# GpSimd weighs five of every eight units of the prior attention, VectorE three, in a fused attention and mixture-of-experts kernel

## What is computed

```python
use_sparse = lam >= SPARSE_THRESHOLD                      # one flag for each of the 2 samples
scores = jnp.einsum('bhqd,bhkd->bhqk', Q, K) * scale
bias = lam[:, None, None, None] * where(prior_mask, 0.0, -1.0)
dense_out = einsum('bhqk,bhkd->bhqd', softmax(scores + bias), V)
...                                                       # the same over 32 listed keys of each query
sparse_out = einsum('bhsk,bhskd->bhsd', softmax(s_scores), Vg)
out = where(use_sparse, sparse_out, dense_out)
```

## Time and profile before

| | us |
|---|---|
| median of 3 runs | 1601.72 |
| lowest and highest | 1598.1, 1601.99 |
| the profiled execution | 1594.84 |
| its span | 1593.0 |

### The profile page before, as it was taken

One profiled execution on the slowest core, in us unless ns is written; L12 is line 12 of the kernel. 1 busy time (PEld: TensorE's weight loads), 2 busy tenths in 40 slices (PEclk: granted clock), 3 DMA queues, 4 the chain that ended last, 5 costly groups with the idle time before them and its releaser, 6 DMA issues. The chain is left out here.

```text
span 1593.0 us, 21701 instructions
## 1 busy us (share of the span) xinstructions
PE 1455.9 (91%) x7649; PEld 693.1 (44%) x7697; DVE 1032.9 (65%) x2506; ACT 810.3 (51%) x975; POOL 666.1 (42%) x455
## 2 busy tenths in 40 slices
PE   4788999999999999888998878799999999999988
PEld 2513333332433332333343323345566567777745
DVE  8789878889767886665877493554451437667232
ACT  3753666787556666457765657733332134334101
POOL 5336799998769999613312012141000300000160
PEclk9759999999999999999999979799999999999999
DMA  2340010231311111113242022130000223544061
GB/s 80 122 132 9 27 41 29 89 80 56 80 34 47 38 39 27 35 35 83 91 115 74 21 71 71 55 101 3 1 0 24 93 70 111 177 153 135 28 121 28
DMA packets 74759, 104.52 MB, mean 66 GB/s; under 512 B 14843, under 2 KB 49092, under 8 KB 74650
## 3 DMA queue, kind: packets, MB, share of 16 engines
q1 hardware_dynamic: 70730, 96.66, 20.1%
q0 software_dynamic: 3072, 6.03, 1.9%
q10 hardware_dynamic: 848, 0.43, 0.1%
HBM read 72.39 MB, written 32.77 MB: 66 GB/s over the span
## 5 line engine op out<-in xcount | busy, mean ns | idle before, releaser
L1475 ACT ACTIVATE sb_prob<-wide,sb_ranges 128x1024 f32<-128x1024 f32 (+3 forms) x384 | 380.1, 1006 | 207.8 <-PE wide L2218 114.5
L1249 POOL TENSOR_TENSOR sb_prob<-sb_prob,sb_weight 128x1024 f32<-128x1024 f32 x192 | 448.9, 2363 | 73.1 <-ACT sb_prob L1475 70.9
L2213 PE MATMUL wide<-sb_stack_q,sb_stack_k 114*128 114x512 f16 (+3 forms) x896 | 282.4, 364 | 15.6 <-ACT sb_prob L1475 7.7
L1799 DVE CUSTOM_DVE_ANT_0 sb_junk<-bank,sb_bias 128x512 bf16<-128x512 f32 x345 | 230.4, 687 | 54.0 <-PE bank L2183 49.2
L1522 ACT ACTIVATE sb_sil<-wide,sb_weight 128x320 f32<-128x320 f32 (+1 forms) x128 | 77.5, 607 | 316.0 <-PE wide L2299 259.1
L2183 PE MATMUL bank<-sb_stack_k,sb_stack_q 112*128 112x512 f16 (+3 forms) x601 | 217.2, 378 | 20.5 <-DVE sb_rowmax L1799 5.7
L2233 PE MATMUL wide<-sb_prob,sb_v_aug 128*17 128x512 f32 (+3 forms) x1792 | 223.6, 564 | 10.3 <-ACT sb_o_raw L1487 8.8
L2299 PE MATMUL wide<-sb_weight,sb_ffn 128*128 128x512 f16 x768 | 181.4, 388 | 9.2 <-DVE sb_act_s L2012 7.3
L2012 DVE SCALAR_TENSOR_TENSOR sb_act_s<-wide,sb_weight,sb_sil 128x512 f32<-128x512 f32 x64 | 47.9, 749 | 186.8 <-ACT sb_sil L1522 172.8
L1254 POOL TENSOR_SCALAR_AFFINE_SELECT sb_prob<-sb_prob 128x256 f32<-128x256 f32 x128 | 53.0, 420 | 244.6 <-ACT sb_prob L1475 244.5
L2183 PEld LDWEIGHTS bank<-sb_stack_k,sb_stack_q 112*128 112x128 f16 x601 | 58.8, 98 | 205.4 <-issue 91.3
(11 more groups left out here) (311 smaller groups left out, 1921.2 us busy)
## 6 DMA issues: line engine op xcount, KB each, us to landing
o_raw<-sb_o_raw SPq DMA_DIRECT2D x32, 256.0 KB, 2.2
sb_weight<-rg SPq DMA_DIRECT2D x8, 1024.0 KB, 4.8
sb_xT<-ru SPq DMA_DIRECT2D x8, 1024.0 KB, 4.8
sb_big<-rd SPq DMA_DIRECT2D x8, 1024.0 KB, 6.2
parts<-sb_o_norm SPq DMA_DIRECT2D x40, 128.0 KB
sb_stack_q<-parts SPq DMA_DIRECT2D x32, 128.0 KB, 3.2
sb_stack_k<-parts SPq DMA_DIRECT2D x32, 128.0 KB, 3.2
sb_o_norm<-o_raw SPq DMA_DIRECT2D x64, 64.0 KB, 2.2
```

The source lines that it names most:

```text
L1249: e.tensor_tensor(p, p, weight_of(*u[1:]), ALU.mult).then_inc(weigh_p.handle, 1)
L1475: e.activation(p[:, :, first:HALF], sc[:, :, first:HALF], ACT.Exp, scale=unscale).then_inc(SC.empty_sem(u), 1)
L1799: e.tensor_tensor_reduce(out=junk[:, i % 2, 0:hi - lo], in0=BK.tile(u)[:, 0:hi - lo], in1=bias[:, qt, lo:hi], scale=1.0, scalar=-3e38, op0 ...
L2213: i = e.matmul(sc[:, j * HALF + first:(j + 1) * HALF], stack_k[0:ROWS_M, n % 3, pair, kt * P:(kt + 1) * P], stack_q[0:ROWS_M, n % 3, PAIRS ...
```

## The change

One tuple changes: which units of every eight are GpSimd's.

```diff
-POOL_UNITS = (0, 1, 3, 4, 5, 7)
+POOL_UNITS = (0, 1, 3, 4, 6)
```

## The result

The changed kernel is slower: 1607.92 us (1604.1 to 1613.28, 8 runs) against 1597.9 us (1591.15 to 1601.99, 8 runs), a ratio of 1.0074 with a 95% interval of 1.0049 to 1.0099. I had forecast 1593.9 and gave "slower" a chance of 0.20. The profiled execution has a span of 1610.1 us, 17.1 more than before. The 8 runs of either kernel spread over 9 to 11 us, so what follows is read from the stage that the change touches, and the whole time only together with its interval.

A forecast was written before the change was run, and what follows sets the result against it. The prediction saw the limit move among GpSimd, TensorE and VectorE by job; 2 - 1 + 0 + 2.5 - 0.3 - 4.0 - 7 = -7.8 us, put on the median 1601.72, gave 1593.9 us, range 1580 to 1610.

The forecast's parts named there:

- The limit of job 0: Job 0, four rounds: VectorE the limit in three, half of 1.14 us lands in each, +2 us.
- the new wait: Scores two units later wait for VectorE's weighing to free the PSUM tile: 0.3 us for each of 32 new units.
- jobs 2 and 6: Job 2 and first three rounds of job 6: limit passes from GpSimd at 14.1 to VectorE at 13.8 with waits, 0.
- the third rival: Rounds with sixteen full maxima: VectorE becomes the bound, its fixed order stalls TensorE; +6 to +15 us, chance 0.22.
- jobs 1 and 5: Eight rounds with TensorE the limit: 0.44 us relief a round against 0.3 for the wait, -1 us.
- job 3: Four rounds: 1.14 us in the round that VectorE fills, 0.5 in the three others, +2.5 us.
- job 4: Same balance as jobs 1 and 5, TensorE busy 16.99 of 17.22 us, in three rounds: -0.3 us.
- the term for GpSimd's pace and the `fin` step: Job 7: GpSimd lets go in first, second and fourth rounds; third round falls from 21.49 to about 14.5 us, -7.
- TensorE's relief: 32 units drop two L2218 matmuls, 0.44 us a round, 14 us in all; worth nothing where VectorE is the limit.
- The `fin` step: Job 7, third round: L1876 finds a gap, -7 us; rival that it stays starved or moves, 1601 us, chance 0.13.
- The sign that it went by: Third rival's threshold: it decides once VectorE's share in a round passes nine tenths, as job 3's 17.16 of 17.22 us.

The follow-up runs named there:

- three even units: Units 2, 4 and 6 of eight to VectorE, five to GpSimd, against the kernel before: 1582.74 us against 1589.36, ratio 0.9962.
- the run with odd places and no more load: Kernel before with units 3 and 7 for VectorE instead of 2 and 6: 1616.29 us against 1589.36, ratio 1.0153.
- the run that changes job 7 alone: Kernel before, but in job 7 units 2, 4 and 6 are VectorE's and five of eight GpSimd's: 1572.61 us against 1587.45, ratio 0.9916.

## Why the prediction was wrong, point by point

**What bounds the kernel.** Right: the changed kernel's GpSimd bounds nothing, and its wait went from 9.1 to 2.5 us. The limit of job 0 I read wrongly: its second round in the earlier trace rows has TensorE at 20.87 of 23.22 us and VectorE at 19.16, and with three even units, so with more work for VectorE, job 0 got 1.5 us shorter.

**The step that failed** is the new wait. It was to cost 0.3 us a unit for 32 units more. I wrote that units 5 and 7 "use the same PSUM tile, but unit 6 between them leaves the same distance as between 2 and 3 before". For the amount of TensorE's work between the scores of a unit and the scores that wait for it, this holds. But the weighing's start is set by what stands in front of it on VectorE, and that maximum comes ahead of the product with V for an even unit and behind it for an odd one. Measured: 0.67 and 0.49 us a unit, and on 64 units, since the change puts both 5 and 7 in new places and takes away unit 6. TensorE's waits for L1910 were to rise to about 20 us and rose to 57.8. I had said in the front part that the product follows every second unit and that `weigh` stands at a fixed place in VectorE's order; I never laid the two side by side for an odd unit. The 0.3 us was a choice between 0.17 and 1.1 and no measurement, and the sum shows it in jobs 1, 5 and 4 only, for 3.3 us; in jobs 2 and 6, where the waits cost most, it stands at nothing. That 1607.92 us lies inside the range of 1580 to 1610 is no merit of the mechanism: the sign was wrong, and the range's upper end came from the third rival.

**The sum, by jobs** (forecast; the change; the same loads at even places):

| | forecast | after | three even units |
|---|---|---|---|
| job 0 | +2 | +3.0 | -1.5 |
| jobs 1 and 5 | -1 | +3.4 | +1.3 |
| jobs 2 and 6 (with its last round, -0.8) | -0.8 | +8.2 | +1.3 |
| job 3 | +2.5 | +2.9 | +2.7 |
| job 4 | -0.3 | +1.5 | -1.0 |
| job 7 | -10.2 | -5.7 | -9.9 |
| prior jobs | -7.8 | +13.3 | -7.1 |

The last column is the kernel nearest to what the forecast assumed: the same loads, waits of 0.11 to 0.23 us a unit. Job 7, the term for GpSimd's pace and the `fin` step, came as summed. Of the others job 0 is off by 3.5 us one way, jobs 1 and 5 and jobs 2 and 6 by 2 us each the other way, so that the two sums, -7.8 and -7.1, agree this well is partly luck. The miss of the change, 21 us against the forecast, is all but wholly the wait. It also ate what GpSimd let go in job 7, where the first round went from 14.00 to 14.53 us instead of the 12.6 that I gave; with even units it is 12.91.

**TensorE's relief.** Of 14 us about 5 were worth something, so my split (worth it where TensorE is the limit, nothing where VectorE is) was the right kind of answer: with the two matmuls back on unit 6, jobs 1, 5, 6 and 7 are 0.9 to 1.8 us longer, of 1.76 at most, and job 3 isn't.

**The third rival** named the right sign and a price, +6 to +15, that holds the measured 10 us. Its mechanism isn't the one. It needed VectorE's load; the run with odd places and no more load lost 24 us, and the changed kernel with one exchange in VectorE's order lost nothing. The sign that it went by, VectorE over nine tenths of a round, isn't enough either: with even units the round of job 2 has VectorE at 13.47 of 14.21 us and is 0.07 us longer than before. Job 3, where VectorE fills a round whole, does lose, 1.9 to 4.1 us in every kernel with five of eight there. A right number for another reason is no hit.

**The `fin` step.** I left open whether its 7 us were chance. They belong to the schedule: 7.18, 6.81 and 7.19 us in three kernels with six of eight, at most 2.24 for that job in all those with five. The forecast of -7 was met by -5.95 in the change and -7.8 in the run that changes job 7 alone. That VectorE is held off by GpSimd's multiplications is seen throughout: in the traces of all eleven kernels, each of the 74 such steps of VectorE that took over 0.3 us ended 65 to 77 ns behind the end of one of them. But an unbroken run isn't enough for 7 us. In job 2 of the kernel before, five multiplications ran without a gap, the fourth ended at 306.99, and the step was through right behind it, although the fifth followed (VectorE's and GpSimd's timelines):

```profile
305.69 1.37 DVE L1876 SCALAR_TENSOR_TENSOR sb_mneg<-sb_mneg,sb_mpart 128x32 f32<-128x32 f32 x1
...
297.67 11.63 POOL L1249 TENSOR_TENSOR sb_prob<-sb_prob,sb_weight 128x1024 f32<-128x1024 f32 x5
```

What differs in the three long cases is GpSimd's backlog: each multiplication that got ahead of the waiting step there had had its exp ready for 2.4 to 3.4 us, since before the multiplication ahead of it began. The last of them in the kernel before, at 641.00, had its exp only at 637.62, 1.4 us after the step had begun. Where the exp had been ready for 0.9 us or less, the step went first, but for two steps that had begun at most 0.06 us before the end of a multiplication and went one later. No run varies the backlog alone, so this is a pattern of the traces and not a cause shown. Taking the step off VectorE and putting it into GpSimd's queue didn't pay: it gave 3.0 us in its round and 0.8 in the job.

Here the Trainium skill was drawn on ("SBUF — State Buffer", section "SBUF: two separate sides"): the lock lasts for one whole instruction. The ends above agree. The trace goes further: L1876 waited 7.18 us through the rest of one multiplication of 2.36 us and three more, so the waiting side can miss several ends of an instruction in turn, and a bound of one or two, as I used it, isn't safe while GpSimd has a backlog.

## What to carry to other kernels

When work moves between engines that run in a fixed order, count the load, and then follow one moved instruction through its own engine's queue: what stands in front of it, and when that gets its input. Two places that look alike from the engine that waits can differ by most of a microsecond, every time; here moving the weighing in front of one maximum took the changed kernel from a ratio of 1.0074 to 0.9971, more than the choice of five or six units at even places was worth. And a split may pay in one part of a stage only: five of eight was worth 8.8 us in the traces in the one job where VectorE had room and GpSimd a backlog, 7.8 of them in the one round with the starved step; over the seven others together, at even places, it cost 2.8 us.

## What was not expected of the hardware

A VectorE instruction of 0.2 us with two inputs in SBUF was on record for 6.8 to 7.2 us beside GpSimd's multiplications, in each of the three kernels in which GpSimd had a backlog there, and for 2.5 us at most everywhere else. While TensorE stood still for its 5.5 us, until 644.06, the granted clock fell from 1.00: it was 0.84 from 636.22 to 643.40 us and 0.61 in the 5.9 us that follow (a window of the kernel before, columns as above). The weighing, with one input in PSUM, took 1.21 to 1.23 us in all these kernels.

```profile
643.40:649.25 5.85, 4.97 (x19) 1.27 (x21) 3.58 (x9) 2.37 (x4) 1.86 (x1) 0.61 0.01 3
```
